# Moving the centring of the next group's weights to GpSimd, and inverting the smoothing factors once

## The reference

```python
ln_out = _ln(hidden_states, ln_w, ln_b)
q = _ln(_fp8_linear_pertensor(ln_out, wq, wq_scale, q_in_scale), qln_w, qln_b)
k = _ln(_fp8_linear_pertensor(ln_out, wk, wk_scale, k_in_scale), kln_w, kln_b)
v = _fp8_linear_pertensor(ln_out, wv, wv_scale, v_in_scale)
core = _gqa(q, k, v)
...
xout = _gqa(qx, kx, vx)
cat = jnp.concatenate([core, xout], axis=-1)
catq = _div_clamp_fp8(cat, proj_smooth)
return jnp.einsum('bsi,oi->bso', catq, wproj) * (proj_in_scale * proj_w_scale)
```

## Time and profile before

| what | value |
|---|---|
| median of 3 runs | 1871.07 us |
| the profiled execution's own time | 1867.37 us |
| its span, first to last instruction | 1865.5 us |
| TensorE busy | 1657.4 us, 89% |
| ScalarE busy | 1406.7 us, 75% |
| VectorE busy | 1383.3 us, 74% |
| GpSimd busy | 1088.3 us, 58% |
| mean granted TensorE clock | 0.971 |

### The profile page before, as it was taken

One profiled execution on the slowest core, in us unless ns is written; L12 is line 12 of the kernel. 1 busy time (PEld: TensorE's weight loads), 2 busy tenths in 40 slices (PEclk: granted clock), 3 DMA queues, 4 the chain that ended last, 5 costly groups with the idle time before them and its releaser, 6 DMA issues. The chain is left out here.

```text
span 1865.5 us, 43325 instructions
## 1 busy us (share of the span) xinstructions
PE 1657.4 (89%) x15491; PEld 1234.2 (66%) x15776; DVE 1383.3 (74%) x3179; ACT 1406.7 (75%) x2936; POOL 1088.3 (58%) x1022
## 2 busy tenths in 40 slices
PE   1449999999999999999999999999997479999998
PEld 1337778778878877887787788778776234444443
DVE  8988988997898899889889988997777422323232
ACT  6659899989989998998999899999999342121211
POOL 1136777777777777777777777777777102020211
PEclk9669999999999999999999999999999799999999
DMA  4027768868877887788778678767889970303000
GB/s 164 25 65 136 134 128 157 149 131 140 143 147 128 143 155 143 130 148 155 125 140 157 130 139 155 154 120 142 160 170 189 264 267 0 136 1 135 0 22 23
DMA packets 640861, 240.29 MB, mean 129 GB/s; under 512 B 612496, under 2 KB 612496, under 8 KB 640656
## 3 DMA queue, kind: packets, MB, share of 16 engines
q1 hardware_dynamic: 640656, 237.62, 62.8%
HBM read 65.57 MB, written 20.97 MB: 46 GB/s over the span
## 5 line engine op out<-in xcount | busy, mean ns | idle before, releaser
L957 POOL TENSOR_TENSOR local<-local 128x512 bf16<-128x512 f32 x512 | 609.2, 1190 | 358.2 <-ACT local L866 358.2
L572 PE MATMUL ps_pj<-wide 128*128 128x256 bf16 (+1 forms) x5544 | 584.5, 254 | 12.8 <-ACT local L789 10.9
L572 PEld LDWEIGHTS ps_pj<-wide 128*128 128x128 bf16 x5544 | 470.0, 98 | 125.9 <-issue 11.7
L863 ACT ACTIVATE local<-ps_s,neg_max 128x512 f32<-128x512 f32 x512 | 390.4, 762 | 62.7 <-DVE neg_max L1165 61.7
L620 PE MATMUL ps_o<-v_hi,local 128*128 128x129 bf16 x2048 | 378.4, 222 | 36.8 <-DMA local<-local 29.1
L866 ACT ACTIVATE local<-ps_s,neg_max 128x512 bf16<-128x512 f32 x512 | 393.0, 768 | 15.0 <-DMA local<-local 15.0
L1165 DVE TENSOR_REDUCE neg_max<-ps_s 128x1 f32<-128x512 f32 x512 | 345.8, 675 | 51.0 <-PE ps_s L636 50.1
L622 PE MATMUL ps_o<-v_hi,local 128*128 128x129 bf16 x2048 | 377.8, 220 | 0.0
L621 PE MATMUL ps_o<-local 128*128 128x128 bf16 x2048 | 377.7, 219 | 0.0
L789 ACT ACTIVATE local<-ps_pj,head_rstd 128x128 f32<-128x128 f32 x756 | 238.9, 436 | 44.1 <-issue 40.4
L620 PEld LDWEIGHTS ps_o<-v_hi,local 128*128 128x128 bf16 x2048 | 199.7, 97 | 52.2 <-DMA local<-local 36.2
(11 more groups left out here) (113 smaller groups left out, 2613.1 us busy)
## 6 DMA issues: line engine op xcount, KB each, us to landing
w_raw<-w_group SPq DMA_DIRECT2D x32, 512.0 KB, 4.2
quantised_heads<-local SPq DMA_DIRECT2D x32, 512.0 KB, 3.2
wide<-quantised_heads SPq DMA_DIRECT2D x4, 4096.0 KB, 14.1
local<-local SPq DMA_TRANSPOSE x640, 3.2
wide<-x SPq DMA_DIRECT2D x8, 1024.0 KB, 11.9
local<-ctx_t SPq DMA_DIRECT2D x4, 1024.0 KB, 5.7
w_raw<-w_proj SPq DMA_DIRECT2D x8, 512.0 KB, 4.3
wide<-w_proj SPq DMA_DIRECT2D x4, 1024.0 KB, 6.2
```

The costliest lines, as they stand in the source:

```text
L572: last = mm(dst[:, at:at + n], lhs, w_at(par, part, c, cross * 512 + at, n), start=(k == 0), stop=(k == len(terms) - 1))
L863: a(p_exp[:, u % 2], ps_s[u % 2][:], ACT.Exp, bias=neg_max[:, u % 4:u % 4 + 1])
L957: tt_(pp[:, u % PP_BUFS, 1], p_exp[:, u % 2], pp[:, u % PP_BUFS, 0], ALU.subtract)\
```

## The change

Four things are edited.

1. The host no longer sends the broadcast smoothing rows. It sends the 4096 factors as 32 more columns of the small table `cols`. VectorE inverts them once at the start (128x32), SP writes the inverses to a tensor in DRAM and reads each group's 512 back, broadcast to 128 rows, at the places of the former loads (the first group's two places later).
2. The reciprocals on the rows, L1151 and L1204, are gone; L1173 waits for the landing of the row.
3. In the groups the centring and scaling of the weights moves from VectorE to GpSimd, in the same slots, behind the low part of the exponentials and ahead of the power. The first group's chunks, in the start, stay on VectorE.
4. The mean is made negative and added, in place of subtracted.

```diff
-            sp.dma_start(rsmooth[:, 0:HEADS * D], smooth_rows[:, 0:HEADS * D]).then_inc(smooth_in, 16)
+            sp.wait_ge(smooth_inverted, 1)
+            sp.dma_start(smooth_dram.rearrange("g (q n) -> (g q) n", n=G * HEADS), inv_smooth[:]).then_inc(smooth_out, 16)
             load_x(2)
             load_weights(2)
+            sp.wait_ge(smooth_out, 16)
+            sp.dma_start(rsmooth[:, 0:HEADS * D], smooth_dram[0].partition_broadcast(P)).then_inc(smooth_in, 16)
...
+            def weight_scale(c, piece, count):
+
+                if piece == 0:
+                    pool.wait_ge(w_step, 2 * count)
+                n = 8 // SCALE_PIECES
+                for h in range(n * piece, min(n * (piece + 1), 7)):
+                    head = raw(c)[:, h * D:(h + 1) * D]
+                    last = nc.gpsimd.tensor_scalar(head, head, w_shift[:, h:h + 1], wscale[:, 8 * c + h:8 * c + h + 1],
+                                                   ALU.add, ALU.mult)
+                if piece == SCALE_PIECES - 1:
+                    last.then_inc(w_scaled, 1)
...
-            v.memset(centre[:], 1.0 / D).then_inc(ones_set, 1)
+            v.memset(centre[:], -1.0 / D).then_inc(ones_set, 1)
...
+            v.reciprocal(inv_smooth[:], c_("smooth", 0, G * HEADS)).then_inc(smooth_inverted, 1)
...
-            dve.wait_ge(smooth_in, 16)
-            v.reciprocal(rsmooth[:, 0:HEADS * D], rsmooth[:, 0:HEADS * D]).then_inc(smooth_ready, 1)
...
                         if u % SLOTS == 0:
-                            dve.wait_ge(smooth_ready, g + u // SLOTS + 1)
+                            dve.wait_ge(smooth_in, 16 * (g + u // SLOTS + 1))
...
-                    if slot == RSMOOTH_SLOT and not last:
-                        dve.wait_ge(smooth_in, 16 * (g + 2))
-                        dve.sem_inc(waited_dve, 1)
-                        rows = rsmooth[:, bass.ds(((g + 1) % 2) * (HEADS * D), HEADS * D)]
-                        v.reciprocal(rows, rows).then_inc(smooth_ready, 1)
```

More of the change, by code:

```diff
@@ L61, with block_kernel @@
                   ("qxln_w", 1), ("qxln_b", 1), ("kln_w", 1), ("kln_b", 1), ("kxln_w", 1), ("kxln_b", 1),
-                  ("s_gate", HC), ("s_up", HC), ("proj_in", 1), ("proj_w", 1)):
+                  ("s_gate", HC), ("s_up", HC), ("proj_in", 1), ("proj_w", 1), ("smooth", G * HEADS)):
     COLS[_name] = (sum(n for _, n in COLS.values()), _n)
 NCOLS = sum(n for _, n in COLS.values())
-def block_kernel(nc, x, ctx_t, w_group, w_proj, w_gate, w_up, w_down, cols, s_down, smooth_rows, out):
+def block_kernel(nc, x, ctx_t, w_group, w_proj, w_gate, w_up, w_down, cols, s_down, out):
     x_tiles = x.rearrange("(b t p) d -> b p t d", b=B, p=P)
@@ L72, in block_kernel @@
     heads_dram = nc.dram_tensor("quantised_heads", (B, G, P, HEADS * T), BF16, kind="Internal").ap()
+    smooth_dram = nc.dram_tensor("inverse_smooth", (G, HEADS * D), F32, kind="Internal").ap()
     stack = ExitStack()
@@ L89, in block_kernel @@
         rsmooth = sb("rsmooth", [P, 2 * HEADS * D], F32)
+        inv_smooth = sb("inv_smooth", [P, G * HEADS], F32)
         ln_scale = sb("ln_scale", [P, SETS * CH], F32)
@@ L106, in block_kernel @@
         w_sum = sb("w_sum", [P, 8], F32)
-        w_mean = sb("w_mean", [P, 8], F32)
+        w_shift = sb("w_shift", [P, 8], F32)
         neg_max = sb("neg_max", [P, 4], F32)
@@ L211, in block_kernel @@
         smooth_in = sem("smooth_in")
-        smooth_ready = sem("smooth_ready")
+        smooth_inverted = sem("smooth_inverted")
+        smooth_out = sem("smooth_out")
         cols_in = sem("cols_in")
@@ L303, in block_kernel @@
         SUMS_LAG, SCALE_LAG, SCALE_PIECES, W_HI_LAG, W_LO_LAG = 2, 6, 2, 10, 11
-        SMOOTH_SLOT, RSMOOTH_SLOT = 22, 31
+        SMOOTH_SLOT = 22
         UNIT_FREE = PV_LAG
@@ L452, in group @@
                         sp.wait_ge(y_done, SLOTS * g + UNIT_FREE)
-                        sp.dma_start(rsmooth[:, bass.ds(((g + 1) % 2) * (HEADS * D), HEADS * D)],
-                                     smooth_rows[:, bass.ds((g + 1) * (HEADS * D), HEADS * D)]).then_inc(smooth_in, 16)
+                        rows = smooth_dram[bass.ds(g + 1, 1)].rearrange("o n -> (o n)").partition_broadcast(P)
+                        sp.dma_start(rsmooth[:, bass.ds(((g + 1) % 2) * (HEADS * D), HEADS * D)], rows).then_inc(smooth_in, 16)
                     for u in unit_at(slot, TURN_LAG, first):
@@ L958, in group @@
                             .then_inc(plo_done, 1)
+                    for piece in range(SCALE_PIECES):
+                        for c in prep_at(slot, SCALE_LAG + 2 * piece, last):
+                            weight_scale(c, piece, CH * g + CH + c + 1)
                     for k in tile_at(slot, VAR_LAG, first, last):
@@ L1007, in weight_sums, with weight_scale_start @@
                 dve.wait_ge(w_step, 2 * count - 1)
[L1008 to L1020, removed]
+                v.tensor_tensor(w_shift[:], w_sum[:], centre[:], ALU.mult).then_inc(w_step, 1)
+            def weight_scale_start(c, count):
+                dve.wait_ge(w_step, 2 * count)
+                for h in range(7):
+                    head = raw(c)[:, h * D:(h + 1) * D]
+                    last = v.tensor_scalar(head, head, w_shift[:, h:h + 1], wscale[:, 8 * c + h:8 * c + h + 1],
+                                           ALU.add, ALU.mult)
+                last.then_inc(w_scaled, 1)
             def weight_lo(par, c, count):
@@ L1113, in weights_centred @@
                 weight_sums(c, c + 1)
-                for piece in range(SCALE_PIECES):
-                    weight_scale(c, piece, c + 1)
+                weight_scale_start(c, c + 1)
             start_norm(0)
@@ L1119, in _ @@
             ln_apply(0, x_at(0), z2)
-            for piece in range(SCALE_PIECES):
-                weight_scale(0, piece, 1)
+            weight_scale_start(0, 1)
             weights_centred(1)
@@ L1186, in group @@
                             .then_inc(heads_done, 1)
-                    for piece in range(SCALE_PIECES):
-                        for c in prep_at(slot, SCALE_LAG + 2 * piece, last):
-                            weight_scale(c, piece, CH * g + CH + c + 1)
                     for c in prep_at(slot, W_LO_LAG, last):
@@ L1285 @@
     w_proj = xa["wproj"].T.reshape(2 * NH, D, DM)[order].reshape(2 * NH * D, DM)
-    smooth = xa["proj_smooth"].reshape(2 * NH, D)[order].reshape(1, 2 * NH * D)
+    smooth = xa["proj_smooth"].reshape(2 * NH, D)[order].reshape(P, G * HEADS)
     def column(v):
@@ L1299 @@
         "s_gate": chunked(ff["s_gate"]), "s_up": chunked(ff["s_up"]),
-        "proj_in": column(xa["proj_in_scale"]), "proj_w": column(xa["proj_w_scale"]),
+        "smooth": smooth, "proj_in": column(xa["proj_in_scale"]), "proj_w": column(xa["proj_w_scale"]),
     }
@@ L1311 @@
         "s_down": np.broadcast_to(ff["s_down"].reshape(1, DM), (P, DM)),
-        "smooth_rows": np.broadcast_to(smooth, (P, 2 * NH * D)),
     }
```

## The result

The changed kernel takes 1908.2 us (1907.27 to 1909.77, 4 runs) against 1871.2, a ratio of 1.0203 (95% interval 1.0191 to 1.0215). It is 37.0 us slower; the forecast was 14.1 us faster, and the range ended at 1892. The prediction was wrong.

A forecast was written before the change was run, and what follows sets the result against it. TensorE, 89% busy, was taken as the bound, waiting most often for GpSimd. Terms -3.3 - 16.3 + 5.5 = -14.1 us took the profiled 1867.37 to 1853.3; against the runs' median, 1857.0 us, range 1846 to 1892.

The forecast's parts named there:

- What bounds the kernel: Whole kernel: TensorE is busy 89%; its largest single wait in the groups is GpSimd's L940, 14.8 us in 1000.
- The reciprocals leave VectorE: Smoothing rows: seven reciprocals in the groups give 16.3 us, the eighth at the start 3.3; 19.6 us gained.
- The scalings leave VectorE: Groups: 196 scalings leave VectorE; no direct TensorE gain counted, at most 5.5 us kept for the low end.
- X: Price of one scaling on GpSimd, taken as 0.26 us from a one-input 128x128 operation at 0.24 us.
- the prediction's own formula: Loss from scalings on GpSimd in the seven groups: 7 x (max(0, 28 X - 8.33) + 3 X).
- I therefore charge nothing as long as 28 X stays below 3.30 + 5.03 = 8.33 us: ScalarE, per group: GpSimd's added 28 X costs nothing up to 8.33 us; anything above is charged in full.
- 5.03 us: ScalarE's waits for neg_max in one group, five together, claimed to vanish and so give room as cover.
- The margins of 3.30 us: Eight gaps per group between the power's end on GpSimd and L789's start on ScalarE, 0.18 to 0.69 us each.
- All of 3 X is added there: Slot 23's L940, behind three scalings in slot 22, comes later by 0.78 us per group; 5.5 us lost.
- head normalisation waits for the power behind the scalings: Rival in GpSimd's queue: X = 0.45, ScalarE waits 4.3 us longer per group; 1891 us, chance 0.20.
- the stretch up to 1980: Rival case of still dearer scalings on GpSimd, outer bound X = 0.86: slower still, up to 1980 us; chance 0.10.
- What stays hidden: Added 128x32 reciprocal at the start and the row read-back, used 125 us after issue: costed at nothing.

The follow-up runs named there:

- e1: Against the changed kernel, the scalings are put back on VectorE; the smoothing factors are still inverted once. 1847.1 us, ratio 0.988.
- e6: e1 with six of the seven scalings of each chunk in the groups left out, so the block is no longer computed; 1840.8 us, ratio 0.9861.
- e5: e1 with three each of scalings with two, one or no columns, other widths, and a tile subtraction in GpSimd's first microseconds; 1851.4 us.
- e2: Against the kernel before, only the scalings move to GpSimd; the reciprocals of the smoothing rows stay on VectorE. 1911.0 us, ratio 1.0221.
- e3: The changed kernel with two loops exchanged: in a slot GpSimd makes the power first, the scalings behind it. 1864.9 us, ratio 0.9977.
- e8: The changed kernel with most scalings behind the power, nine of a group's 28 in quiet GpSimd slots, and each chunk's last earlier; 1847.2 us.

## Why the prediction was wrong, point by point

- **What bounds the kernel: seen, but not weighed.** It saw that TensorE waits for GpSimd most often, and that L789 follows the power with 0.18 to 0.69 us to spare.
- **The reciprocals leave VectorE, 19.6 us: right.** e1 gained 21.9. Its first neg_max comes 3.3 us earlier. ScalarE's wait of 1.54 us is gone, and that of 1.68 is down to 0.97.
- **The scalings leave VectorE, at most 5.5 us: about right.** e6 shows 4.5 to 6.3 for six sevenths.
- **"I take X = 0.26": mis-sized, the first failure.** It is 0.43. The row that it came from has no columns to read, and e5 measured 0.27 for a scaling with none; the two columns, named as the reason why 0.24 was a lower end, cost 0.16 and got 0.02. With X = 0.434 (85.0 us over 196) the prediction's own formula gives a loss of 7 x (12.15 - 8.33 + 1.30) = 35.9 us, not 5.5, and a time of 1887. So the price alone turns the sign, but doesn't reach 1908.
- **"I therefore charge nothing as long as 28 X stays below 3.30 + 5.03 = 8.33 us": the second failure.** Both terms of this cover were too large, and together 4.0 us were hidden. Of the 5.03 us, the reciprocals' share had been booked already, as TensorE's 16.3 us: it was counted twice. The prediction gave them two of the waits, 1.54 and 1.68; e1 shows that of the second only 0.71 was theirs, since 0.97 are still there. What the move of the scalings itself took off these waits is the 2.5 us per group above. e2 shows the same from the other side: the reciprocals' waits and the scalings' lie in the same slots, so one hides the other instead of paying for it. The margins of 3.30 us weren't there in full either. ScalarE's wait for the power rose by 10.7 us per group for 12.15 us of scalings, so 1.5 were hidden, and eight rings with 0.19 us of slack each give 1.5. A margin before one instruction is not the slack of the ring that it belongs to. As an estimate, with 4.0 us hidden even the price of 0.26 would have lost 7 x (7.28 - 4.0) = 23 us on ScalarE alone, more than the 19.6 gained.
- **"All of 3 X is added there", 5.5 us for L940 at slot 24: the wait came, but not beside the others.** TensorE waits 2.23 us there where it was 0.52. Added to the corrected cover it would make 7 x (12.15 - 4.0 + 1.30) = 66 us, and 59 to 61 are measured, of which ScalarE's waits alone give 57. So little of it can lie beside them.
- **The rival** "head normalisation waits for the power behind the scalings" was the right mechanism, with X = 0.45 nearly the right price. The prediction had it at 0.20. Its 1891 us rests on the same cover of 8.33; the measured time lies in the stretch up to 1980 that had 0.10 and was left out of the range.
- **What stays hidden: right.** The added reciprocal and the read-back cost nothing that e1 would show.

What is still open: how the 18 us that e3 leaves divide, and how much of the remaining 5 to 6 us could be had with both engines sharing the scalings without a wait in VectorE's queue. The second wasn't tried.

## What to carry to other kernels

GpSimd idled for 42% of the span, and that hid little of the work put on it; what hid work was the slack of the ring that its queue belongs to. So close the ring in the timeline (who releases whom until the same instruction comes again), subtract it from the period, and place the new work behind the instruction that the ring waits for: against the same work on VectorE, the 196 operations cost some 60 us ahead of the power, 18 behind it, and at most 2 in slots chosen for them. A wait that one part of a change removes may be counted once, as time or as cover, never as both.

Price an operation by what it reads, not by its shape: a column of factors counted here for as much as 100 elements.

The best versions found are e1 and, within 2 us, e8: the smoothing factors inverted once, at 1847 us, 1.2% below the kernel before.

## What was not expected of the hardware

On GpSimd a per-partition column cost 0.07 to 0.09 us of each 128x128 scaling that read one (e5), so seven narrow scalings of 128 columns spend 7 x 0.16 = 1.1 of their 3.0 us on reading factors. A subtraction of two 128x128 tiles took 0.41 us, little less than a scaling of one by two columns.
